# Input statistics by half, a fold in two parts, bias products behind layer one, and half of the second FFN matrix quantised by GpSimd

## The reference

```python
xn = (x - mean) / sqrt(var + 1e-5)                      # per token, over 256 channels
q, k, v = [gelu(xn @ W1n + b1n) @ W2n + b2n for n in "qkv"]   # exact gelu, 256 -> 256 -> 256
s = (q @ k.T) / sqrt(256 * 512) * tril(ones)            # no softmax
s = layernorm(s @ v) * ln_w + ln_b
Wq = clip(round(W / (mean(abs(W)) + 1e-5)), -1, 1)      # for both FFN matrices: values -1, 0, 1
f = relu(xn @ Wq1.T + b1) @ Wq2.T + b2                  # 256 -> 1024 -> 256
out = x + s * silu(f)
```

## Time and profile before

| what | value |
|---|---|
| median of 3 runs | 324.38 us (322.96 to 326.89) |
| the profiled execution | 323.89 us, its span 322.2 us |
| PE busy | 307.6 us, 95% of the span |
| DVE busy | 273.7 us, 85% |
| ACT busy | 212.3 us, 66% |
| POOL busy | 132.5 us, 41% |
| chain that ended last | PE 87%, DVE 7%, ACT 3% |

### The profile page before, as it was taken

The page is one execution under the profiler, slowest core; times in us unless marked ns, Lnnn a source line. Parts: engine busy times, 40 slices in busy tenths (PEclk is TensorE's granted clock), DMA queues, the critical chain, the costliest instruction groups (busy, mean ns, idle before and its releaser), DMA issues.

```text
span 322.2 us, 5816 instructions
## 1 busy us (share of the span) xinstructions
PE 307.6 (95%) x1850; PEld 273.9 (85%) x1850; DVE 273.7 (85%) x680; ACT 212.3 (66%) x338; POOL 132.5 (41%) x107
## 2 busy tenths in 40 slices
PE   7996799999999999999999999999999999999990
PEld 6874699889998899888998899888998899988990
DVE  3799867999779987999779987899779997897697
ACT  2899344697538964698538973699537983599330
POOL 2031643418272472518262371616443272600453
PEclk9999599999999999999999999999999999999997
DMA  7943540230003200130004200221003200010001
GB/s 241 369 151 90 182 145 1 78 119 1 2 0 130 66 0 0 65 126 5 0 0 130 66 0 0 65 95 36 0 0 130 66 0 0 0 66 0 0 1 65
DMA packets 15769, 20.07 MB, mean 62 GB/s; under 512 B 1936, under 2 KB 12688, under 8 KB 15760
## 3 DMA queue, kind: packets, MB, share of 16 engines
q1 hardware_dynamic: 15200, 19.17, 18.5%
q10 hardware_dynamic: 560, 0.80, 0.7%
HBM read 15.74 MB, written 4.22 MB: 62 GB/s over the span
## 4 chain that ended last, share of the span: by engine, by line
PE 87%; DVE 7%; ACT 3%; issue 1%; POOL 0%; DVEq 0%; POOLq 0%
PE bank L683 85%; PE bank L675 1%; DVE g_lo L502 1%; DVE s_lo L586 1%; DVE w2q L477 1%; ACT r_lo L332 1%; ACT bank L358 1%; DVE gw L606 0%; ACT g_hi L357 0%; DVE s L474 0%; DVE x_all L614 0%; DVE o_stats L602 0%; DVE x_stats L428 0%; ACT L357 0%; ACT xT_hi L345 0%
## 5 line engine op out<-in xcount | busy, mean ns | idle before, releaser
L357 ACT ACTIVATE g_hi<-bank,col 128x512 fp32r<-128x512 f32 x48 | 33.2, 693 | 24.1 <-PE bank L683 24.1
L367 ACT ACTIVATE r_hi<-bank,col 128x512 fp32r<-128x512 f32 x64 | 48.6, 760 | 0.0
L368 ACT ACTIVATE bank<-bank,col 128x512 f32<-128x512 f32 x64 | 47.3, 739 | 0.0
L531 DVE TENSOR_TENSOR r_lo<-bank,r_hi 128x512 fp32r<-128x512 f32 x64 | 40.0, 682 | 3.9 <-ACT bank L368 3.9
L287 POOL TENSOR_TENSOR y<-y,row 128x512 f32<-128x512 f32 (+1 forms) x17 | 21.0, 1236 | 50.4 <-DVE gw L556 50.4
L683 PE MATMUL bank<-xT_lo,w1q 128*128 128x512 f32 x128 | 40.0, 394 | 0.2 <-DVE d_weight L492 0.2
L683 PE MATMUL bank<-xT_hi,w1q 128*128 128x512 f32 x128 | 39.8, 392 | 0.0
L271 POOL TENSOR_TENSOR y<-y,xn 128x512 f32<-128x512 f32 x14 | 23.3, 1662 | 39.1 <-DMA xn<-x_norm_rows 39.1
L683 PE MATMUL bank<-w2q,r_lo 128*128 128x256 f32 x256 | 35.4, 281 | 0.0
L683 PE MATMUL bank<-w2q,r_hi 128*128 128x256 f32 x256 | 34.9, 279 | 0.0
L683 PEld LDWEIGHTS bank<-w2q,r_lo 128*128 128x128 f32 x256 | 32.7, 189 | 0.7
(11 more groups left out here) (114 smaller groups left out, 721.4 us busy)
## 6 DMA issues: line engine op xcount, KB each, us to landing
out<-x_all SPq DMA_DIRECT2D x15, 256.0 KB, 2.2
x_all<-in_x SPq DMA_DIRECT2D x7, 512.0 KB, 3.6
y<-in_x_t SPq DMA_DIRECT2D x7, 512.0 KB, 3.4
xn<-x_norm_rows SPq DMA_DIRECT2D x7, 512.0 KB, 3.7
x_all<-in_w1t SPq DMA_DIRECT2D x1, 1024.0 KB, 7.3
x_all<-in_w2t SPq DMA_DIRECT2D x1, 1024.0 KB, 11.7
row<-in_rows ACTq DMA_DIRECT2D x1, 512.0 KB, 7.2
x_all<-in_x ACTq DMA_DIRECT2D x1, 256.0 KB, 3.7
```

The lines of the kernel that those rows point to most:

```text
L357: nc.scalar.activation(g["hi"][:, m], pre[:], ACT.Gelu, bias=b1)
L367: nc.scalar.activation(r["hi"][:, f], pre[:], ACT.Relu, bias=b1)
L368: nc.scalar.activation(pre[:], pre[:], ACT.Relu, bias=b1).then_inc(f1_whole, 1)
L531: nc.vector.tensor_tensor(r["lo"][:, f], bank[(AT_F1 + f) % BANKS][:], r["hi"][:, f].bitcast(FP32), ALU.subtract).then_inc(r_split, 1)
```

## The change

It has five parts, all in batch 0.

1. Input: batch 0 is loaded in four pieces instead of two; mean and variance are computed for tiles 0 and 1 and then for tiles 2 and 3, with a power on POOL for each half.
2. Fold: PE does the first half of the fold, transposes 0 and 1, the second half, transposes 2 and 3.
3. Bias products: moved from ahead of layer one to behind `m` = 1. ACT rounds the second matrix (`weight_hi(1, 1)`) after `xT_hi` instead of before.
4. FFN thresholds: the sum for the first matrix is moved from behind `m` = 1 to behind `m` = 3. That for the second goes from f = 4 to f = 1, and PE waits for `thr_made` 4 there. On DVE the first matrix is quantised by halves of the 1024 outputs, and then come the statistics of batch 1 and `thresholds(1)`, all ahead of the first `g_lo`.
5. Second matrix: DVE quantises one half after the second `r_lo`; POOL quantises the other with three operations (`quantise_rest`), written ahead of the x_rstd of batch 1.

Three operations of 1024 elements stand ahead of the power that batch 1's normalisation starts from. The diff, cut to its core:

```diff
-        GAMMA = (bank[4][:, 0:1], bank[5][:, 0:1])
+        GAMMA = (bank[7][:, 8:9], bank[7][:, 9:10])
...
+            sp.dma_start(x_all[:, 0, 0], x[0, 0:P]).then_inc(x0_loaded[0], 16)
+            sp.dma_start(x_all[:, 0, 2], x[0, 2 * P:3 * P]).then_inc(x0_loaded[2], 16)
...
             sp.wait_ge(w1_quantized, 2)
-            sp.wait_ge(w2_quantized, 2)
+            sp.wait_ge(w2_quantized, 1)
+            sp.wait_ge(w2_rest_quantized, 1)
...
-            x_rstd_of(0)
+            for h in range(2):
+                half = slice(2 * h, 2 * h + 2)
+                pool.wait_ge(x0_var_made[h], 1)
+                nc.gpsimd.tensor_tensor(x_rstd[:, half], x_var[:, half], neg_half[:, half],
+                                        ALU.pow).then_inc(x0_rstd_made[h], 1)
             pool.wait_ge(qkv_loaded[5], 16)
             nc.gpsimd.tensor_copy(w["hi"][:, 4], raw_qkv[:, 5]).then_inc(w2v_hi_made, 1)
             pool.wait_ge(w2v_hi_made, 1)
             nc.gpsimd.tensor_tensor(w["lo"][:, 4], raw_qkv[:, 5], w["hi"][:, 4].bitcast(FP32),
                                     ALU.subtract).then_inc(w2v_split, 1)
+            def quantise_rest():
+                rest = slice(FT // 2, FT)
+                pool.wait_ge(thr_made, 4)
+                nc.gpsimd.tensor_scalar(less, raw2[:, rest], neg_thr[:, 1:2], None, ALU.is_lt).then_inc(less_made, 1)
+                nc.gpsimd.tensor_scalar(w2q[:, rest], raw2[:, rest], thr[:, 1:2], None, ALU.is_gt).then_inc(more_made, 1)
+                pool.wait_ge(less_made, 1)
+                pool.wait_ge(more_made, 1)
+                nc.gpsimd.tensor_tensor(w2q[:, rest], w2q[:, rest].bitcast(FP32), less,
+                                        ALU.subtract).then_inc(w2_rest_quantized, 1)
+            quantise_rest()
...
+            act.dma_start(x_all[:, 0, 1], x[0, P:2 * P]).then_inc(x0_loaded[1], 16)
+            act.dma_start(x_all[:, 0, 3], x[0, 3 * P:T]).then_inc(x0_loaded[3], 16)
...
             weight_hi(0, 0)
-            weight_hi(1, 1)
             act.dma_start(row[:], rows.rearrange("(o r) c -> o r c", o=1).broadcast_to((P, 4, C))).then_inc(rows_loaded, 16)
             for k in range(CK):
                 act.wait_ge(xT_summed, k + 1)
                 nc.scalar.copy(xT["hi"][:, k], bank[AT_X0 + k][:]).then_inc(xT_hi_made, 1)
+            weight_hi(1, 1)
...
-                    if first and m == 2:
+                    if first and m == 1:
...
+            def x_statistics0():
+                for h in range(2):
+                    for t in (2 * h, 2 * h + 1):
+                        dve.wait_ge(x0_loaded[t], 16)
+                        nc.vector.bn_stats(x_stats[:, t], x_all[:, 0, t]).then_inc(x0_stats_made[h], 1)
+                    aggregate(x_stats, x_part, x_mean, x_var, x0_stats_made[h], 2, x0_var_made[h],
+                              slice(2 * h, 2 * h + 2))
...
+            x_statistics0()
+            x_normalise0()
             split_weight(0)
+            xT_lo(0, [bank[AT_X0 + k][:] for k in range(CK)])
             split_weight(1)
-            xT_lo(0, [bank[AT_X0 + k][:] for k in range(CK)])
-            dve.wait_ge(consts_made, 4)
-            nc.vector.tensor_copy(ones_r[:], ones[:]).then_inc(ones_rounded, 1)
...
-            def quantise(n, raw, quant, done):
-                dve.wait_ge(thr_made, 2 * n + 2)
-                for h in range(2):
-                    part = slice(h * F, (h + 1) * F)
-                    if n or h:
-                        dve.wait_ge(done if h else w1_quantized, 1 if h else 2)
-                    nc.vector.tensor_scalar(flags, raw[:, part], neg_thr[:, n:n + 1], None,
-                                            ALU.is_lt).then_inc(flags_made, 1)
-                    dve.wait_ge(flags_made, 2 * n + h + 1)
-                    nc.vector.scalar_tensor_tensor(quant[:, part], raw[:, part], thr[:, n:n + 1], flags,
-                                                   ALU.is_gt, ALU.subtract).then_inc(done, 1)
+            def quantise(raw, quant, n, scratch, done):
+                nc.vector.tensor_scalar(scratch, raw, neg_thr[:, n:n + 1], None, ALU.is_lt).then_inc(flags_made, 1)
+                dve.wait_ge(flags_made, done[1])
+                nc.vector.scalar_tensor_tensor(quant, raw, thr[:, n:n + 1], scratch,
+                                               ALU.is_gt, ALU.subtract).then_inc(done[0], 1)
             dve.wait_ge(fold_hi_made, 1)
             nc.vector.tensor_tensor(w["lo"][:, 3].rearrange("p k c -> p (k c)"), bank[6][:],
                                     w["hi"][:, 3].rearrange("p k c -> p (k c)").bitcast(FP32),
                                     ALU.subtract).then_inc(fold_read, 1)
             split_weight(2)
-            thresholds(0, GAMMA[0])
-            quantise(0, raw1, w1q[:].rearrange("p a b -> p (a b)"), w1_quantized)
+            dve.wait_ge(consts_made, 4)
+            nc.vector.tensor_copy(ones_r[:], ones[:]).then_inc(ones_rounded, 1)
             dve.wait_ge(folded, 2)
             nc.vector.tensor_copy(z_bias[:], FOLD_Z)
             nc.vector.tensor_copy(d_const[:], FOLD_D)
             nc.vector.tensor_copy(d_weight[:], FOLD_DW).then_inc(fold_read, 1)
+            thresholds(0, GAMMA[0])
+            dve.wait_ge(thr_made, 2)
+            for h in range(2):
+                if h:
+                    dve.wait_ge(w1_quantized, 1)
+                part = slice(h * (F // 2), (h + 1) * (F // 2))
+                quantise(raw1[:, :, part], w1q[:, :, part], 0, flags.rearrange("p (k f) -> p k f", k=CK), (w1_quantized, h + 1))
+            x_statistics(1, second=True)
+            thresholds(1, GAMMA[1])
...
-                if first:
-                    x_statistics(1, second=True)
                 dve.wait_ge(e_made, i + 1)
                 nc.vector.tensor_copy(e["hi"][:], e32[:]).then_inc(e_hi_made, 1)
                 dve.wait_ge(e_hi_made, i + 1)
                 nc.vector.tensor_tensor(e["lo"][:], e32[:], e["hi"][:].bitcast(FP32), ALU.subtract).then_inc(e_split, 1)
-                if first:
-                    thresholds(1, GAMMA[1])
-                    quantise(1, raw2, w2q[:].rearrange("p a b -> p (a b)"), w2_quantized)
                 for f in range(FT):
+                    if first and f == 2:
+                        dve.wait_ge(thr_made, 4)
+                        dve.wait_ge(w1_quantized, 2)
+                        quantise(raw2[:, 0:FT // 2], w2q[:, 0:FT // 2], 1, flags.rearrange("p (f c) -> p f c", c=C),
+                                 (w2_quantized, 3))
...
-            def fold_weights():
-                for n in (3, 4):
-                    pe.wait_ge(qkv_loaded[n], 16)
-                for n in range(CK):
-                    last = split_product(bank[6][:, n * C:(n + 1) * C],
-                                         [(w2kT[:, k, n * P:(n + 1) * P], w2qT[:, k]) for k in range(CK)])
-                last.then_inc(folded, 1)
+            def fold_weights(n):
+                return split_product(bank[6][:, n * C:(n + 1) * C],
+                                     [(w2kT[:, k, n * P:(n + 1) * P], w2qT[:, k]) for k in range(CK)])
...
                     if first and m == 1:
+                        fold_biases()
+                    if first and m == 3:
+                        pe.wait_ge(fold_read, 2)
                         sum_partitions(0)
-                    if first and m == 3:
-                        pe.wait_ge(thr_made, 2)
-                if first:
-                    pe.wait_ge(fold_read, 2)
-                    pe.wait_ge(w1_quantized, 2)
                 for f in range(FT):
-                    if first and f == 4:
-                        pe.wait_ge(g_split, 6)
+                    if first and f % (FT // 2) == 0:
+                        pe.wait_ge(w1_quantized, 2 * f // FT + 1)
+                    if first and f == 0:
+                        pe.wait_ge(fold_read, 1)
+                    if first and f == 1:
                         sum_partitions(1)
-                    if first and f == 7:
                         pe.wait_ge(thr_made, 4)
...
                 if first:
-                    pe.wait_ge(w2_quantized, 2)
+                    pe.wait_ge(w2_quantized, 1)
+                    pe.wait_ge(w2_rest_quantized, 1)
...
-            fold_weights()
-            transpose_x0()
-            fold_biases()
+            for n in (3, 4):
+                pe.wait_ge(qkv_loaded[n], 16)
+            fold_weights(0)
+            transpose_x0((0, 1))
+            fold_weights(1).then_inc(folded, 1)
+            transpose_x0((2, 3))
             batch(0, first=True)
```

More of the change, by code:

```diff
@@ L133, in gated_block @@
         flags_made, w1_quantized, w2_quantized = sem("flags_made"), sem("w1_quantized"), sem("w2_quantized")
+        less_made, more_made, w2_rest_quantized = sem("less_made"), sem("more_made"), sem("w2_rest_quantized")
         x_stats_made, x_var_made, x_rstd_made, xn_made = (
             sem("x_stats_made"), sem("x_var_made"), sem("x_rstd_made"), sem("xn_made"))
```

(37 more changed lines are left out.)

16 lines of the change are left out of this document (7 added, 9 removed).

## The result

The changed kernel takes 327.66 us (median of 4 runs, 326.46 to 330.47), the kernel before 323.67 beside it: ratio 1.0146, 95% interval 1.0112 to 1.0180. That is 4.0 us slower by the medians and 4.7 by the ratio; a ratio here is not exactly that of the medians. Forecast was 322.9, 1.5 faster. The result lies within 2%, but on the other side, and above the range of 320.0 to 327.2. The profiled execution took 327.9 us, its span 326.2 against 322.2.

What follows compares the result with a forecast made beforehand. PE, busy 95%, bounds the kernel through batch 1's start. Batch 1 starting 2.6 earlier, less 0.8 given back, with a likely clock dip, gave -1.5: profiled 323.9 to 322.4, median 322.9; range 320.0 to 327.2.

Steps and rivals of the forecast that it cites:

- What bounds the kernel, and 5.9 us as the most to gain: PE sets the time through batch 1's start; stall and low clock ahead of and in K cost 5.9 us.
- Start, fold, transposes: 0: Start of batch 0: the same PE matmuls in another order fill the same time; 0 us.
- Bias products: +0.8: Layer one: moved products no longer cover ACT's rounding of the transposed input; its end comes at 21.9, +0.8 us.
- First matrix: 0: Ahead of the first FFN layer: first quantised half ready at 21.55, before PE comes at 21.9; no wait.
- The new wait: 3.1: First FFN layer: PE waits for the second matrix's thresholds from 23.0 to 26.1, +3.1 us.
- K and V: the old stall goes, -2.6: K starts at 33.4 at full clock, V at 36.65 instead of 39.23; batch 1 starts at 54.85, -2.6 us.
- POOL's three operations: 4.5: POOL's quantising of half the second matrix: 4.5 us taken, from a low-to-high span of 4.5 to 7.4.
- high bound of 7.4: Upper price for POOL's three quantising operations, each taken at 2.40 like a two-input operation of this width; 7.4 us.
- Batch 1: +0.8 back: Inside batch 1: DVE, 1.8 us later relative to PE against 1.0 slack, gives back +0.8 us as short waits.
- The first rival: POOL slower, 2.4 us per operation: its chain makes O wait; 325.5, or 327.9 with the clock lost; 20%.
- The second rival: More of the stall comes back: no clock dip, DVE's lag vanishes in slack; -2.6 to -4, about 321; 14%.
- The third: Shared port makes each `g_lo` wait while POOL works, V follows at 41; +1.5, about 326; 8%.

Runs made afterwards that it cites:

- The best version: Kernel before, with both halves of the second matrix quantised on DVE behind the second `r_lo`: 321.49 us, ratio 0.9918.
- 324.15: Changed kernel with POOL copying its half of the second matrix instead of quantising it (result not the reference's): 324.15 us, ratio 1.0011.

## Why the prediction was wrong, step by step

- **What bounds the kernel, and 5.9 us as the most to gain:** not contradicted. The best version took 4.4 of them in its profile (batch 1 at 53.05 against 57.40) and 2.4 to 2.7 over all its runs.
- **Start, fold, transposes: 0.** Failed in the mechanism, by 0.45 us in the end. I wrote that PE's work covers the earlier steps and did not ask what the added loads do to W2k: it came late, and the fold started at 7.61 instead of 6.25. That the added loads are the cause is likely by the means above (7.27 against 6.54) and not shown. Fold and transposes then took 2.8 us instead of 3.8, which gave most of it back by luck; layer one started 0.45 later than forecast.
- **Bias products: +0.8.** The size stands where the clock stays up: with two loads the fold started at 6.25 and FFN step 0 at 21.97, forecast 21.9. The clock in layer one was not in the sum: m = 2 from 16.57 took 2.7 us instead of 1.4, and m = 3 took 1.7. FFN step 0 started at 24.02.
- **First matrix: 0.** Right: no wait of PE for it.
- **The new wait: 3.1.** Measured 2.85, at the named place. The clock did not fall there in this execution; in the six other kernels with the stall it did, so a dip more likely than not was a fair call.
- **K and V: the old stall goes, -2.6. This step failed most.** Its 0.7 us for "one clash with POOL's power" was 2.9: `e_hi` and `e_lo` took 4.0 us instead of 1.05. The rule was at hand. The Trainium skill (SBUF — State Buffer, two separate sides) says that the second to issue blocks fully, and I wrote that by it `e_hi` and `e_lo` clash; the trace agrees, with `e_lo` at 2.75 against 0.69. But I had POOL done at 30.6, before them. With a compare at 2.86 it was not. PE stood 2.82 us more, the clock fell, V started at 41.77, forecast 36.65 to 37.95. V came 5.12 us later than 36.65: 1.97 were there when the wait for the thresholds ended (28.07 against 26.1), 2.26 more when K started (37.63 against 33.4), with `e_hi` and `e_lo`, and 0.89 went in K at the low clock. What such a clash costs stood in the trace of the kernel before, in two lines that my rows leave out: DVE's second compare-and-subtract for the first matrix took 2.21 us instead of 1.28 beside POOL's split of W2v.

```profile
18.61 2.21 DVE L477 SCALAR_TENSOR_TENSOR w1q<-x_all,thr,s 128x1024 fp32r<-128x1024 f32 x1
18.11 1.62 POOL L262 TENSOR_TENSOR w_lo<-raw_qkv,w_hi 128x512 fp32r<-128x512 f32 x1
```

- **POOL's three operations: 4.5.** This is the term that the step above rests on. Measured 8.2 (28.11 to 36.34), outside even my high bound of 7.4; without these operations `e_hi` and `e_lo` take their own 0.41 and 0.69 and 3.5 of the 4.0 us are back. The bound took the nearest row by width, a subtraction of two tensors, and the form asked about was dearer than that. The GPSIMD Engine Reference of the Trainium skill (4.1, Engine selection) gives about line rate for one input; that agrees with the copy (1.04) and not with this form (2.86).
- **Batch 1: +0.8 back.** Measured 1.46. The scores were split at 57.1, forecast 51.4: 2 us of that is the start, 3.7 POOL.
- **The first rival**, POOL late, had the mechanism: O waiting for `s_lo` shows at full size (7.3 us) where PE is early, and in the change only as the floor under it, since PE was late by then too. It named the chain and left out the port. Its number with the clock lost, 327.9, is near the 327.66 measured, by luck: the loss came by K and batch 1's waits and not at O. My range stopped at 327.2, below that branch.
- **The second rival** did not come. **The third**, each `g_lo` held, is refuted: six `g_lo` took their usual time (31.04 to 32.91 for the last three) beside a compare of POOL.

What stays open is how the 1.3 us between 324.15 and the forecast split among W2k, the clock and DVE's half beside POOL, for each is of the size of the runs' spread. In the profile of that kernel FFN step 0 came 2.05 us later than forecast (23.95), PE waited 2.83 us for the thresholds with the clock falling at about 27.6, and DVE's half took 4.2 us instead of 2.03.

## What to carry to other kernels

Work moved to GpSimd is not free because GpSimd is idle: price it by a row of the same form of instruction, ask what stands behind it in its own queue, and lay it over the stretches in which VectorE works on two SBUF inputs, or copies or compares from SBUF to SBUF. Here there was one window of almost 6 us, while the means travel through DRAM, in which VectorE can quantise undisturbed, and the gain lay in filling that window and in letting two small operations go first. A bound from the nearest row is no bound when the form is another; leave room above it.

## What the runs showed of the hardware

- On GpSimd, TENSOR_SCALAR takes 2.77 to 2.86 us for 1024 elements and 1.57 for 512, a two-tensor operation 2.34, a copy 1.04, with no other engine at work. On VectorE the same compare takes 0.75.
- Beside a working GpSimd, VectorE's compare from SBUF to SBUF took up to 2.74 us instead of 0.75, its compare-and-subtract up to 2.59 instead of 1.28, and a cast of 512 elements up to 1.65 instead of 0.42, by how they overlapped, while subtractions with one input in PSUM kept their time (six `r_lo` in 3.67). GpSimd loses too: a compare took 3.41 instead of 2.86 (in the kernel before with only POOL's half), a normalising operation up to 2.58 instead of 1.6.
- A stall's length alone doesn't tell the clock: in the changed kernel 2.85 us (25.2 to 28.1) left it up and 2.82 ahead of K brought it down; 2.85 in the same place brought it down with two loads; and the 3.7 us ahead of K lowered it 1.6 us after their start in the kernel before, and only 0.9 us after their end with the bias products moved.
- The first four matmuls of the fold took 1.10 us from 7.61 in the changed kernel and 2.05 from 7.64 with the second matrix all on DVE, though nothing differs between the two up to there and the profile gives the full clock for both. Layer one started 1.9 us apart (11.50 and 13.37). Why is open, and a profile of one execution can differ from the next by that much.
